# Interleaving scores and weighted context with the key banks, 128-column loads, and two banks squared whole

## The reference

```python
def rmsnorm(x, g, eps=1e-5):
    var = jnp.mean(jnp.square(x), axis=-1, keepdims=True)
    return x * jax.lax.rsqrt(var + eps) * g
q = (hidden_states @ Wq).reshape(B, Sq, H, D)            # layernorm(x), B=8, Sq=64, H=16, D=128
k = (encoder_hidden_states @ Wk).reshape(B, Skv, H, D)   # ctx, Skv=1601
v = (encoder_hidden_states @ Wv).reshape(B, Skv, H, D)
q = rmsnorm(q, gq)
k = rmsnorm(k, gk)
scores = jnp.einsum('bqhd,bkhd->bhqk', q, k) * scale
attn = jax.nn.softmax(scores, axis=-1)
out = jnp.einsum('bhqk,bkhd->bqhd', attn, v)
x = x + out.reshape(B, Sq, H * D) @ Wo                   # then attention and ternary ffn
```

## Time and profile before

| | |
|---|---|
| time, median of 3 runs | 1642.44 us (1640.22 to 1644.5) |
| the profiled execution | 1639.37 us, span 1637.5 us |
| TensorE busy | 1522.4 us, 93%, weight loads 1171.6 us |
| VectorE busy | 1233.7 us, 75% |
| ScalarE busy | 1005.8 us, 61% |
| GpSimd busy | 173.1 us, 11% |
| mean granted TensorE clock | 0.977 |

### The profile page before, as it was taken

The page is one execution under the profiler, slowest core; times in us unless marked ns, Lnnn a source line. Parts: engine busy times, 40 slices in busy tenths (PEclk is TensorE's granted clock), DMA queues, the critical chain, the costliest instruction groups (busy, mean ns, idle before and its releaser), DMA issues.

```text
span 1637.5 us, 21762 instructions
## 1 busy us (share of the span) xinstructions
PE 1522.4 (93%) x6872; PEld 1171.6 (72%) x6872; DVE 1233.7 (75%) x1949; ACT 1005.8 (61%) x3683; POOL 173.1 (11%) x121
## 2 busy tenths in 40 slices
PE   6969999999999999999999999999999876997898
PEld 5756667777777777777777777777677655885687
DVE  7635778778877977797788778867977896767543
ACT  4555677666676766766667767677666564622442
POOL 2210000002000200020020002000200202012343
PEclk9989999999999999999999999999999988997999
DMA  5531112111111121121122112111110241650000
GB/s 168 163 128 43 55 51 83 36 41 55 62 37 38 54 68 35 35 87 35 36 61 64 37 34 63 61 36 38 55 39 26 72 138 55 208 206 2 1 1 26
DMA packets 85074, 103.66 MB, mean 63 GB/s; under 512 B 31704, under 2 KB 67040, under 8 KB 83168
## 3 DMA queue, kind: packets, MB, share of 16 engines
q1 hardware_dynamic: 77664, 94.94, 18.6%
q10 hardware_dynamic: 7296, 7.34, 1.3%
HBM read 80.24 MB, written 22.02 MB: 62 GB/s over the span
## 4 chain that ended last, share of the span: by engine, by line
PE 74%; DVE 16%; issue 4%; ACT 3%; POOL 1%; DMA 1%; ACTq 0%; DVEq 0%; SPq 0%; POOLq 0%
PE ps L35 24%; PE ps L36 22%; PE ps L37 22%; PE ps L695 2%; PE ps L696 2%; DVE p_lo L41 2%; DVE run_sum L933 2%; DVE k_step L873 1%; PE ps L713 1%; PE ps L714 1%; DVE fq_lo L41 1%; DVE ring L888 1%; DVE ring L913 1%; DVE cn_lo L41 1%; PE ps L452 1%
## 5 line engine op out<-in xcount | busy, mean ns | idle before, releaser
L1328 ACT ACTIVATE ps<-ps 123x128 f32<-123x128 f32 (+1 forms) x1248 | 330.3, 265 | 293.0 <-PE ps L37 292.9
L35 PE MATMUL ps<-wk_hi,cT_hi 128*123 128x512 f32 (+1 forms) x832 | 341.5, 410 | 21.0 <-ACT w_scale L1400 10.9
L36 PE MATMUL ps<-wk_lo,cT_hi 128*123 128x512 f32 (+1 forms) x832 | 329.3, 396 | 0.0
L37 PE MATMUL ps<-wk_hi,cT_lo 128*123 128x512 f32 (+1 forms) x832 | 328.9, 395 | 0.0
L1328 ACT ACTIVATION_READ_ACCUMULATOR ps<-ps 123x1 f32 (+1 forms) x1248 | 233.8, 187 | 0.0
L35 PEld LDWEIGHTS ps<-wk_hi,cT_hi 128*123 128x123 f32 (+1 forms) x832 | 153.8, 185 | 109.7 <-ACT ps L1328 54.5
L35 PE MATMUL ps<-p_hi,cn_hi 123*128 123x512 f32 (+1 forms) x416 | 174.8, 420 | 30.7 <-DVE cn_lo L41 27.8
L862 DVE TENSOR_REDUCE k_sum<-sq 123x4 f32<-123x512 f32 (+1 forms) x104 | 71.0, 683 | 150.4 <-ACT sq L1322 150.4
L37 PEld LDWEIGHTS ps<-wk_hi,cT_lo 128*123 128x123 f32 (+1 forms) x832 | 153.9, 185 | 39.4
L36 PEld LDWEIGHTS ps<-wk_lo,cT_hi 128*123 128x123 f32 (+1 forms) x832 | 154.4, 186 | 28.7
L35 PE MATMUL ps<-fq_hi,cT_hi 128*123 128x512 f32 (+1 forms) x416 | 165.6, 398 | 7.1 <-DVE ring L888 6.9
(11 more groups left out here) (198 smaller groups left out, 2690.4 us busy)
## 6 DMA issues: line engine op xcount, KB each, us to landing
cT_raw<-in_ctxT SPq DMA_DIRECT2D x88, 123.0 KB, 2.2
cn_raw<-in_ctx SPq DMA_DIRECT2D x88, 123.0 KB
w_raw<-in_wguT SPq DMA_DIRECT2D x32, 256.0 KB, 2.8
qk_scratch<-folded ACTq DMA_DIRECT2D x8, 896.0 KB, 4.1
fq_raw<-qk_scratch SPq DMA_DIRECT2D x7, 1024.0 KB, 5.0
ternary_scratch<-w_out SPq DMA_DIRECT2D x48, 128.0 KB, 1.7
pc_scratch<-pc_out SPq DMA_DIRECT2D x6, 1024.0 KB, 7.2
w_bf<-ternary_scratch SPq DMA_DIRECT2D x1, 6144.0 KB, 22.9
```

Source lines behind the costliest of these rows:

```text
L35: pe.matmul(dst, l_hi, r_hi, start=first, stop=False)
L36: pe.matmul(dst, l_hi, r_lo, start=False, stop=False)
L37: return pe.matmul(dst, l_lo, r_hi, start=False, stop=last)
L1328: done = act.activation(head, head, ACT.Square, accum_out=k_sum[0:n, i, g * GH + h:g * GH + h + 1])
```

## The change

- TensorE: in step s, S0 of tile s - 1 follows K0, S1 follows K1, A0 of tile v follows K2, and A1 follows K3 (in a step with ternary work behind the ternary matmul). Scores are one tile later than before.
- The loads of cT take 128 columns for every tile (the rows behind a tile's 123 or 124 are those of the next tile, and nobody reads the results); cT_hi and cT_lo have three buffers instead of two.
- ScalarE squares banks 1 and 3 whole into `sq`, which is twice as large, and banks 0 and 2 per head; VectorE's one reduce sums both.
- The lists of ScalarE, VectorE and GpSimd are in another order: key_mean(s) is last in VectorE's step, key_refine(s - 1) in the next, low_cT(s + 1) behind the maximum, GpSimd's sum ahead of its maximum.

```diff
@@ -432,15 +433,14 @@
             def key_bank(s, g):
-                b, t, n = tiles[s]
-                kb, cols, i = g % 2, slice(g * BANK, (g + 1) * BANK), s % 2
+                kb, cols, i = g % 2, slice(g * BANK, (g + 1) * BANK), s % 3
                 if g == 0:
                     pe.wait_ge(cT_lo_done, s + 1)
                 if s == 0 and g == 0:
                     pe.wait_ge(wk_lo_done, KC * NG)
                 pe.wait_ge(*free[kb])
                 for k in range(KC):
-                    done = products(pe, bank(kb)[0:n], cT_hi[:, i, k, 0:n], cT_lo[:, i, k, 0:n],
+                    done = products(pe, bank(kb), cT_hi[:, i, k], cT_lo[:, i, k],
                                     wk_hi[:, k, cols], wk_lo[:, k, cols], k == 0, k == KC - 1)
                 done.then_inc(keys_mm, 1)
                 free[kb] = (k_squared, NG * s + g + 1)
...
@@ -452,51 +452,51 @@
 
-            def scores(s):
+            def scores(s, half):
                 b, t, n = tiles[s]
-                i = s % 2
-                if t == 0:
-                    pe.wait_ge(fq_lo_done, KC * (b + 1))
-                if s > 0:
-                    pe.wait_ge(scaled, s)
+                i, hh = s % 3, slice(half * BANK, (half + 1) * BANK)
+                if half == 0:
+                    if t == 0:
+                        pe.wait_ge(fq_lo_done, KC * (b + 1))
+                    if s > 0:
+                        pe.wait_ge(scaled, s)
+                for k in range(KC):
+                    done = products(pe, bank(S_BANK + half), cT_hi[:, i, k], cT_lo[:, i, k],
+                                    fq_hi[:, k, hh], fq_lo[:, k, hh], k == 0, k == KC - 1)
+                if half == 1:
+                    done.then_inc(scores_mm, 1)
+
+            def weighted_context(v, c2):
+                b, t, n = tiles[v]
+                if c2 == 0:
+                    pe.wait_ge(p_lo_done, v + 1)
+                    pe.wait_ge(cn_lo_done, v + 1)
+                if t == 0 and b > 0:
+                    pe.wait_ge(evacuated, evacuations(b - 1, c2) if b - 1 < B - 2 else evacuations(b - 1))
+                cc = slice(c2 * P, (c2 + 1) * P)
                 for half in range(2):
                     hh = slice(half * BANK, (half + 1) * BANK)
-                    for k in range(KC):
-                        done = products(pe, bank(S_BANK + half)[0:n], cT_hi[:, i, k, 0:n], cT_lo[:, i, k, 0:n],
-                                        fq_hi[:, k, hh], fq_lo[:, k, hh], k == 0, k == KC - 1)
-                done.then_inc(scores_mm, 1)
-
...
+                    done = products(pe, bank(AV_BANK + c2 * 2 + half), cn_hi[0:n, v % 2, cc], cn_lo[0:n, v % 2, cc],
+                                    p_hi[0:n, v % 2, hh], p_lo[0:n, v % 2, hh], t == 0, t == TT - 1)
+                done.then_inc(av_mm, 1)
 
             for s in range(N + LAG_AV):
                 v = s - LAG_AV
-                if s < N:
-                    for g in range(NG):
+                for g in range(NG):
+                    if s < N:
                         key_bank(s, g)
-                    if s == 0:
-                        for c in range(KC):
-                            fold(NG - 1, c)
-                    else:
-                        if s == 1:
-                            scores(0)
-                        scores(s)
-                    if s in piece_at:
+                    if g < 2 and 1 < s <= N:
+                        scores(s - 1, g)
+                    if g == 3 and s in piece_at:
                         ternary_groups(piece_at[s])
-                if v >= 0:
-                    weighted_context(v)
+                    if g >= 2 and v >= 0:
+                        weighted_context(v, g - 2)
+                if s == 0:
+                    for c in range(KC):
+                        fold(NG - 1, c)
+                if s == 1:
+                    for half in range(2):
+                        scores(0, half)
 
 
...
@@ -841,10 +841,8 @@
             def low_cT(s):
-                n = tiles[s][2]
                 dve.wait_ge(cT_hi_done, s + 1)
-                low_part(dve, cT_lo[:, s % 2, :, 0:n], cT_raw[:, s % 3, :, 0:n],
-                         cT_hi[:, s % 2, :, 0:n]).then_inc(cT_lo_done, 1)
+                low_part(dve, cT_lo[:, s % 3], cT_raw[:, s % 3], cT_hi[:, s % 3]).then_inc(cT_lo_done, 1)
 
             def low_cn(s):
...
@@ -859,8 +857,9 @@
             def key_mean(s):
                 i, n = s % 2, tiles[s][2]
                 dve.wait_ge(k_squared, NG * (s + 1))
-                dve.tensor_reduce(k_sum[0:n, i, (NG - 1) * GH:], sq[0:n].rearrange("p (h d) -> p h d", h=GH),
-                                  AX_X, ALU.add).then_inc(k_summed, 1)
+                odd = k_sum[0:n, i].rearrange("p (a r h) -> p a r h", a=2, r=2)[:, :, 1]
+                dve.tensor_reduce(odd, sq[0:n].rearrange("p a (h d) -> p a h d", h=GH), AX_X, ALU.add).then_inc(
+                    k_summed, 1)
                 dve.wait_ge(k_summed, s + 1)
                 dve.tensor_scalar(k_mean[0:n, i], k_sum[0:n, i], 1.0 / HD, LN_EPS,
...
@@ -989,37 +988,37 @@
             low_cT(0)
             for s in range(N + LAG_AV):
                 u, v = s - LAG_P, s - LAG_AV
-                key, num, av = s < N, 0 <= u < N, 0 <= v < N
+                scored, num, av = 0 <= s - 1 < N, 0 <= u < N, 0 <= v < N
                 if s == 0:
                     for c in range(KC):
                         fold_copy(NG - 1, c)
                     low_fq(0)
-                if 0 <= s - 1 < N:
-                    scale_scores(s - 1)
-                    if 1 < s < N and tiles[s][1] == 0:
-                        low_fq(tiles[s][0])
-                    if tiles[s - 1][1] == TT - 1:
-                        track_max(s - 1)
-                if num:
+                if num and tiles[u][1] > 0:
                     subtract_max(u)
-                if v > 0 and tiles[v][1] == 0:
-                    sum_refine(tiles[v][0] - 1)
+                if av and v > 0 and tiles[v][1] == 0:
                     evacuate(tiles[v][0] - 1)
                 if av:
                     numerator_lo(v)
                     low_cn(v)
-                if 0 <= s - 1 < N and tiles[s - 1][1] != TT - 1:
-                    track_max(s - 1)
-                if key:
-                    key_mean(s)
+                if num and tiles[u][1] == 0:
+                    subtract_max(u)
+                if scored:
+                    key_refine(s - 1)
                 if num:
                     track_sum(u)
+                if scored:
+                    scale_scores(s - 1)
+                    track_max(s - 1)
+                if s > 1 and s < N and tiles[s][1] == 0:
+                    low_fq(tiles[s][0])
                 if s + 1 < N:
                     low_cT(s + 1)
-                if key:
-                    key_refine(s)
                 if s in piece_at:
                     ternary_round(piece_at[s])
+                if av and tiles[v][1] == TT - 1:
+                    sum_refine(tiles[v][0])
+                if s < N:
+                    key_mean(s)
                 if s == N + 3:
                     for head in range(NH3):
...
@@ -1291,11 +1289,10 @@
                 return ring[0:tiles[s][2], s % RING]
 
             def high_cT(s):
-                n = tiles[s][2]
                 act.wait_ge(cT_in[s % 3], 16 * (s // 3 + 1))
-                if s >= 2:
-                    act.wait_ge(scores_mm, s - 1)
-                act.copy(cT_hi[:, s % 2, :, 0:n], cT_raw[:, s % 3, :, 0:n]).then_inc(cT_hi_done, 1)
+                if s >= 3:
+                    act.wait_ge(scores_mm, s - 2)
+                act.copy(cT_hi[:, s % 3], cT_raw[:, s % 3]).then_inc(cT_hi_done, 1)
 
             def high_cn(s):
...
@@ -1316,10 +1313,10 @@
             def key_square(s, g):
                 i, n = s % 2, tiles[s][2]
                 act.wait_ge(keys_mm, NG * s + g + 1)
-                if g == NG - 1:
-                    if s > 0:
+                if g % 2:
+                    if g == 1 and s > 0:
                         act.wait_ge(k_summed, s)
-                    act.activation(sq[0:n], bank(g % 2)[0:n], ACT.Square).then_inc(k_squared, 1)
+                    act.activation(sq[0:n, g // 2], bank(g % 2)[0:n], ACT.Square).then_inc(k_squared, 1)
                     return
                 if g == 0 and s >= 2:
...
@@ -1347,11 +1344,13 @@
                     act.wait_ge(av_mm, KC * (u - 1))
                 act.copy(p_hi[0:tiles[u][2], u % 2], ring_slot(u)).then_inc(p_hi_done, 1)
 
-            def sum_guess(b):
+            def sum_log(b):
                 act.wait_ge(sum_spread, b + 1)
                 if b > 0:
                     act.wait_ge(evacuated, evacuations(b - 1))
                 act.activation(recip[:], col_sum[:], ACT.Ln).then_inc(sum_guessed, 1)
+
+            def sum_guess(b):
                 act.wait_ge(sum_guessed, 2 * b + 1)
```

(54 more changed lines are left out.)

29 lines of the change are left out of this document (7 added, 22 removed).

## The result

| | before | after |
|---|---|---|
| median | 1642.23 us (1640.22 to 1644.5) | 1669.55 us (1665.62 to 1671.31, 4 runs) |
| ratio, 95% interval | | 1.0163 (1.0139 to 1.0186) |
| profiled execution | 1639.37 us | 1668.49 us, span 1666.7 |
| TensorE busy | 93% | 91% |
| mean granted clock | 0.977 | 0.964 |

The change makes the kernel 27.3 us slower. The forecast had the sign and the main mechanism (1653 us), but not the size, and the time lies 2.6 us over its range.

The account below looks back on a forecast made before the run. TensorE, 93% busy with weight loads waiting 54.5 us for ScalarE's squares, bounds the loop. Start -4.2, steps 2 to 13 +4.6, steps 14 to 103 +5.3, end +4.6: together +10.3, 1642.4 to 1653 us; range 1618 to 1667.

Parts of the forecast that it names:

- start, to K0(2): Loop start: step 2's first matmul comes at about 127.9 instead of 132.13, -4.2 us, of which 2.7 is only moved.
- steps 2 to 13: Early steps, including ten ternary ones without context at 10.07 us each: 122.8 us against 118.2, +4.6.
- step 14: Step behind the first change of batch: counted as a plain 10.90 us less 2.7 for having no context.
- six changes, with s = 79 and 92: Later changes of batch: 2 x 7.4 + 4 x 8.8 = 50 us, plus 4.2 for ternary work in steps 79 and 92.
- end: Behind step 103, to the last batch's second-tile sum: 27.4 us against 22.8, +4.6 including the moved 2.7.
- 48 x 0.227 = 10.90 us: Plain step on TensorE: 48 matmuls at the pitch of a 128-column load, giving back 0.36 us a step.
- Rival 4: Matmul pitch on TensorE stays 0.232: 17 us more, 1670 us; chance 0.12 together with rival 3.
- The change of batch: GpSimd's reductions hold VectorE, cT_lo comes 4.5 or 7.2 us late; half clock then costs TensorE 2.9 or 1.6 us.
- rival 3: GpSimd's reductions hold scale_scores on VectorE as well: 7 x 1.14 = 8 us, 1661 us; chance 0.12 together with rival 4.
- rival 2: Pauses at changes of batch come but the clock stays at 2.4 GHz: 12 us less, 1641 us, no change; chance 0.13.
- Rival 1: Holds at changes of batch hardly matter, costing no more than the earlier 2.4 us: 35 us less, 1618 us; chance 0.25.
- The ternary step: Later steps with ternary work: 0.27 us late squares beside the ternary matmul's 0.24, 0.51 us in each of 35.

Follow-up runs that it names:

- experiment 7: The changed kernel with matmuls loading only the tile's own 123 or 124 columns again, transfers and splits still at 128: 1678.26 us, ratio 1.0211 to the kernel before.
- (8): The changed kernel with both halves of the weighted context at the end of TensorE's step: 1660.82 us, ratio 1.01 to the kernel before.
- Experiment 3: The changed kernel with key_mean and the sum's refinement ahead of the six ternary operations on VectorE: 1647.75 us, ratio 1.0036 to the kernel before.
- experiment 5: The changed kernel with 16, later 24, unread matmuls filling TensorE's pause behind each change of batch: 1661.45 us, ratio 1.0105 to the kernel before.
- (1): The changed kernel with cT_lo(s+1) right behind the running sum, ahead of scale_scores: 1660.96 us, ratio 1.012 to the kernel before.
- (2): The changed kernel with GpSimd's maximum all-reduce ahead of its sum, as before the change: 1671.03 us, ratio 1.018 to the kernel before.
- (9): Experiment 3's kernel with, at changes of batch only, cT_lo ahead of the running sum and fq_lo ahead of track_max: 1632.03 us, ratio 0.9927 to the kernel before.
- (11): The changed kernel with both GpSimd all-reduces cut to 16 of 1024 columns, part of the computation left out: 1624.50 us, ratio 0.9905 to the kernel before.
- (12): The kernel before with both GpSimd all-reduces cut to 16 of 1024 columns, part of the computation left out: 1617.12 us, ratio 0.9856 to the kernel before.

## Why the prediction was right in kind and wrong in size

Against the profiled execution the forecast was 1649.7 us; 1668.5 came. The 18.8 us by the prediction's own steps:

| step of the prediction | forecast | measured | off by |
|---|---|---|---|
| start, to K0(2) | 127.9 | 128.84 | +0.9 |
| steps 2 to 13 | 122.8 | 123.0 | +0.2 |
| step 14 | 8.2 | 14.5 | +6.3 |
| 89 plain steps, 15 to 103 | 10.90 each | 10.99 each | +8.0 |
| 35 steps with ternary work | 0.51 each | 0.47 each | -1.4 |
| six changes, with s = 79 and 92 | 54.2 | 57.4 | +3.2 |
| step 15, half clock a second time | 0 | 1.7 | +1.7 |
| end | 27.4 | 27.1 | -0.3 |

- "**48 x 0.227 = 10.90 us**" failed in size. It took the pitch for a matter of columns. It is one in part: at 123 columns the step is 11.12 (experiment 7). But at 128 columns each turn between groups of 128 and of 123 rows costs 0.03 us too (8), and the change makes four turns where there were two. The kernel before could have told: in the earlier trace rows context at 0.227 stands for a group behind another of its kind as well as for 128 columns; only the second reading was used. Rival 4 (the pitch stays 0.232) is wrong too, though half its price was due; that its 1670 us meets the measured time is chance.
- **Step 14** failed outright. The forecast let only 2.7 us for the missing context fall away. Step 14 has ternary work and no context, like steps 3 to 12, for which the prediction itself added 1.9 us to the same 8.2; for step 14 it left them out. It had the ternary operations ahead of key_mean, but not that one of them waits for a store, and not that the first change's short wait (1.52 us) comes on top of TensorE's wait for squares (1.93 us) and brings the clock down: 5.4 us of step 14 run at half clock, which costs 2.7 us by the forecast's own way of counting. The late key_mean then makes ScalarE late, TensorE waits 2.81 us for w_scale, and the clock falls a second time (step 15). Experiment 3, with key_mean ahead of that store, takes 2.6 us off steps 14 and 15 and the second half clock with them. The 1.9 left out, the 2.7 and the 1.5 that experiment 3 takes off step 14 make about the 6.3 us.
- **The change of batch** was right: who of the two-input operations is held, who isn't (scale_scores, rival 3 refuted by the 1.22 us at s = 39), the order in which cT_lo comes, a pause of 6.8 us where 7.2 was forecast and 3.4 us where it was 4.5, the half clock (rival 2 refuted). What rival 2 says for itself, that the clock held behind pauses of 2.3 us before, was true of two of five: in the kernel before the clock was 0.50 for 3.4 or 3.5 us around pauses of 2.68, 2.70 and 2.26 us (from 404.7, 558.3 and 1152.3), and full around pauses of 2.28 and 2.29 us. Rival 1, that a hold is dodged, happened at none of the six later changes (run_max took 3.89 to 4.54 us at each). Within the term two sizes were off and in part cancel: the clock costs 8 to 9 us (experiment 5), not 12; steps 80 and 93, behind the ternary work of 79 and 92, take 15.86 and 17.68 us, 4.4 and 6.2 over a ternary one, not 2.1, for sum_refine's 2.5 us stands ahead of key_mean there as well (in step 93 the clock falls too, 1199.4 to 1206.2).
- **The ternary step** was right in size and cause: with key_mean first only the ternary matmul's 0.24 us is left.
- The rows say that holds are moved rather than removed: 3.3 us onto run_max (s = 52), 4.4 onto cT_lo (1) or w_scale (2), 3.4 onto fq_lo (9), each time up to 4.4 or 4.5 us behind the sum reduction's start. Their position makes them cost 31 instead of 17 us in the loop, 14 of the 33 us by which the changes got dearer. The other 19 are there without holds, 26 us (11) against 8 (12). In 11 they lie at four late cT_lo (7 us) and in steps 80 and 93 (12 us), where key_mean stands behind ternary work and sum_refine, which is the new order on VectorE. Moving key_mean (3) and then cT_lo and fq_lo (9) takes 21 us off the changes, holds included; the two parts were not tried apart.

The upper end was 2.6 us too low: the 8 us of the pitch alone lay inside it, the 8 us around the first change beside them did not.

## What to carry to other kernels

Before reordering an engine that is 75% busy, write down for each of its results when it is wanted, and put behind the last wanted one everything that can wait for somebody else: here two lines (key_mean ahead of the ternary work) were worth 21.8 us of a 27.3 us loss. A hold by another engine falls on the next operation that can be held, so it has to be given one whose result has slack; swapping the holders alone gave nothing. With both done, the interleaving is 0.7% faster than the kernel before instead of 1.6% slower.

## What the runs showed of the hardware that was not expected

- Six matmuls of 512 columns, nothing waited for, go at 0.227 us each if the group ahead loads from as many rows, and at 0.231 to 0.232 if not (1.36 and 1.39 us a group, 128 and 123 rows here, the rows not parted from what else differs); with 123 instead of 128 columns loaded in the key and score groups all eight groups go at 0.231 to 0.233.
- An all-reduce over 1024 columns holds VectorE for part of its time only: the sum's takes 6.11 us and lets run_max end 0.5 us ahead of it (701.79 + 4.54 against 700.72 + 6.11), so that with its 1.23 us of work it began some 1.7 us ahead of the reduction's end; the maximum's 3.8 to 4.1 us cost fq_lo 1.7. Spans on GpSimd are rough in the profile.
- One-input tensor_scalar operations are held as well: w_scale in bf16, 4.66 us instead of 0.29 (2), and k_mean in f32, 0.85 us instead of 0.17 (9, at 699.93).
- A fill that ends 1.3 us before the pause does kept the clock at its 2.4 GHz level at four changes, where a pause of 6.8 us had lost it. Much shorter pauses can lose it too: behind 3.37 us (changed kernel, s = 26 and 39), behind 2.36 us at three changes of four (9), and around 2.26, 2.68 and 2.70 us but not 2.28 and 2.29 us in the kernel before. What tells these apart stays open.
